# One-head attention on Trainium2: the second context of each pair turned whole on TensorE, the first loaded in both layouts, and the first transfers sent inside the norm

## What is computed

```python
x = x + _L0_xattn_ref(_layernorm(x), ctx_1024, ctx_1024, Wq, bq, Wk, bk, 32, 0)

q = einsum('bld,ed->ble', query, Wq) + bq
k = einsum('bld,ed->ble', key, Wk) + bk
scores = einsum('bqd,bkd->bqk', q, k) / 32
attn = softmax(scores, axis=-1)
return einsum('bqk,bkd->bqd', attn, value)      # key = value = ctx_1024
```

## Time and profile before

| | us |
|---|---|
| median of 3 runs | 3767.55 |
| lowest, highest | 3767.08, 3770.37 |
| the profiled execution | 3748.75 |
| its span (first to last instruction) | 3747.0 |
| mean granted TensorE clock of it (share of full speed) | 0.948 |
| one-head stage in it, from the span's start to the last `add` | 209.5 |

### The profile page before, as it was taken

How to read it: one execution, slowest core, us unless ns; L and a number is a source line. 1 busy time by engine, 2 the same in 40 slices (tenths; PEclk the granted TensorE clock), 3 DMA queues, 4 the chain that set the end, 5 groups by cost and what they waited for, 6 DMA issues and landing times. The chain is left out here.

```text
span 3747.0 us, 96803 instructions
## 1 busy us (share of the span) xinstructions
PE 3314.1 (88%) x40678; PEld 2442.0 (65%) x40678; DVE 2529.9 (68%) x3627; ACT 2085.7 (56%) x3878; POOL 1150.4 (31%) x1140
## 2 busy tenths in 40 slices
PE   8786999999999678999999984689999999999989
PEld 5565677777777566777777762456666666666654
DVE  4653777777774346777777756578878787878751
ACT  3421566556664124656666654366777777676733
POOL 0024222222221352212222200145555545454530
PEclk8987999999999788999999997799999999999989
DMA  7934665565562336545455510100000000000000
GB/s 199 241 101 131 163 172 153 150 173 146 157 173 53 98 103 147 119 122 138 120 123 138 127 44 0 32 25 17 25 17 26 17 25 17 25 17 25 17 4 24
DMA packets 136408, 337.82 MB, mean 90 GB/s; under 512 B 56515, under 2 KB 78603, under 8 KB 135979
## 3 DMA queue, kind: packets, MB, share of 16 engines
q1 hardware_dynamic: 132843, 325.21, 33.6%
q0 software_dynamic: 3136, 6.46, 0.5%
HBM read 166.49 MB, written 17.17 MB: 49 GB/s over the span
## 5 line engine op out<-in xcount | busy, mean ns | idle before, releaser
L2148 POOL TENSOR_TENSOR l_S<-l_S,l_shift 125x448 f32<-125x448 f32 (+1 forms) x416 | 461.3, 1152 | 328.7 <-ACT l_shift L2380 326.2
L1464 ACT ACTIVATE L1a_probs<-ps 125x448 f32<-125x448 f32 x768 | 383.3, 544 | 204.1 <-PE ps L1364 190.6
L1464 ACT ACTIVATE L2a_probs<-ps 125x448 f32<-125x448 f32 x768 | 382.6, 544 | 203.2 <-PE ps L1364 189.6
L1497 DVE TENSOR_REDUCE L2a_chunk_max<-ps 112x1 f32<-112x1000 f32 x256 | 300.9, 1196 | 148.0 <-PE ps L1323 147.6
L1497 DVE TENSOR_REDUCE L1a_chunk_max<-ps 112x1 f32<-112x1000 f32 x256 | 300.9, 1196 | 137.3 <-PE ps L1323 136.8
L2361 ACT ACTIVATE ctx_stats<-ps 125x512 f32<-125x512 f32 (+1 forms) x416 | 247.9, 596 | 179.7 <-PE ps L2206 170.5
L2258 PE MATMUL ps<-l_S,l_z 125*128 125x448 f32 x768 | 344.2, 545 | 0.0
L2425 DVE TENSOR_REDUCE l_norms<-ctx_stats 125x8 f32<-125x512 f32 (+1 forms) x416 | 268.2, 676 | 77.1 <-ACT ctx_stats L2361 77.0
L2451 DVE SCALAR_TENSOR_TENSOR l_S<-ps,l_neg_cols,l_inv_norms 125x448 f32<-125x448 f32 x384 | 256.3, 680 | 81.4 <-PE ps L2227 76.5
L1323 PE MATMUL ps<-L1a_keys,L1a_queries 98*112 98x500 f32 x768 | 264.9, 428 | 47.5 <-DVE L1a_chunk_max L1497 20.8
L1323 PE MATMUL ps<-L2a_keys,L2a_queries 96*112 96x500 f32 x768 | 264.1, 426 | 46.3 <-DVE L2a_chunk_max L1497 20.7
(11 more groups left out here) (494 smaller groups left out, 7074.0 us busy)
## 6 DMA issues: line engine op xcount, KB each, us to landing
L1a_keys<-L1a_k_hi SPq DMA_DIRECT2D x256, 187.5 KB
L2a_keys<-L2a_k_hi SPq DMA_DIRECT2D x256, 187.5 KB, 3.7
L1a_ctx_T<-in_ctx_T SPq DMA_DIRECT2D x32, 750.0 KB, 6.3
xn<-L_valid SPq DMA_DIRECT2D x32, 750.0 KB, 7.8
L1a_keys<-L1a_k_lo SPq DMA_DIRECT2D x128, 187.5 KB
L2a_ctx_T<-in_ctx_T SPq DMA_DIRECT2D x32, 750.0 KB, 6.4
L2a_keys<-L2a_k_lo SPq DMA_DIRECT2D x128, 187.5 KB, 4.1
a_ctx_N<-in_ctx_N SPq DMA_DIRECT2D x32, 672.0 KB
```

The costliest lines, as they stand in the source:

```text
L1464: nc.scalar.activation(probs[t % NPR][:, h * HQ // 2:(h + 1) * HQ // 2], s.ps[0:KP, i % 3, 0:HQ // 2], ACT.Exp).then_inc(probs_made, 1)
L1497: ins = nc.vector.tensor_reduce(chunk_max[:, n, 0:1], product, AX.XY, ALU.max)
L2148: nc.gpsimd.tensor_tensor(S[b % 2][0:r, t, :], S[b % 2][0:r, t, :], shift[0:r, :], ALU.add)\
```

## The change

Three things change in `attention_one_head`.

The first batch of a pair (2j) is loaded in both layouts, `ctx_T` whole (750 KB). Of the second batch (2j+1) only `ctx_N` is loaded; its `ctx_T` is made on the chip whole, in three turns of four tiles, `turn_context(j, k)` for k = 0, 1, 2, each with its copy `take_context(j, k)`. All turns still go through bank 7, so each waits for the copy of the one before it. TensorE makes turn 0 of pair j+1 behind `mix(j-1)`, turn 1 behind `turn_probs(j)` and turn 2 behind `turn_out(j-1)`, just ahead of `scores(j+1)`. ScalarE copies turn 0 behind the exponentials, and turns 1 and 2 behind the three `probs_T` copies. Every chunk of scores now waits for its copy.

Turn 0 of pair j+1 now needs `ctx_N` of batch 2j+3, which SyncE sends last of its pair; before, it needed that of batch 2j+2.

The first contexts are sent from inside the norm's block (`on_sync`) and no longer from the block ahead of it, batch 1's `ctx_N` before batch 0's.

```diff
@@ -287,7 +287,6 @@
 
     PAIRS, NB, NBN = B // 2, 4, 6
-    LOADED = KT - KT // NKC
     QP = 64
     TG = KT // NKC
     with ExitStack() as ctx:
@@ -323,8 +322,7 @@
             sem(n) for n in ("probs_turned", "turned_taken", "mixed", "scaled", "out_turned", "added", "stats_made"))
 
         def load_T(sp, b):
-            sp.dma_start(ctx_T[b % NB][:, 0:LOADED, :],
-                         a["ctx_T"][b, :, 0:LOADED * KP].rearrange("d (t p) -> d t p", t=LOADED))\
+            sp.dma_start(ctx_T[b % NB][:, :, :], a["ctx_T"][b].rearrange("d (t p) -> d t p", t=KT))\
                 .then_inc(T_loaded[b % NB], 16)
 
         def load_N(sp, b):
@@ -338,14 +336,17 @@
                 for dst, src in ((wq[:, :], "L0_WqT"), (wk[:, :], "L0_Wk"), (bias[:, 0:1], "L0_bq"),
                                  (bias[:, 1:2], "L0_bk")):
                     sp.dma_start(dst, a[src]).then_inc(weights_loaded, 16)
-                for b in range(2):
-                    load_T(sp, b)
-                    load_N(sp, b)
 
...
-        norm()
+
+        def load_first(sp):
+            load_T(sp, 0)
+            load_N(sp, 1)
+            load_N(sp, 0)
+
+        norm(on_sync=load_first)
 
         batches = ExitStack()
         block = batches.enter_context(nc.Block())
@@ -355,8 +356,7 @@
             for j in range(1, PAIRS):
                 if j >= 2:
                     sp.wait_ge(scores_made, (j - 2) * NKC + NKC)
-                for b in (2 * j, 2 * j + 1):
-                    load_T(sp, b)
+                load_T(sp, 2 * j)
                 if j >= 3:
                     sp.wait_ge(mixed, j - 3 + 1)
                     sp.wait_ge(stats_made, (j - 2) * 2 * KT)
@@ -380,17 +380,14 @@
             mm.then_inc(qbk_made, 1)
 
             def scores(j):
-                for u in range(2):
-                    b = 2 * j + u
-                    pe.wait_ge(T_loaded[b % NB], 16 * (b // NB) + 16)
+                pe.wait_ge(T_loaded[2 * j % NB], 16 * (2 * j // NB) + 16)
                 if j == 0:
                     pe.wait_ge(qbk_taken, 1)
                     pe.wait_ge(qk_taken, NCH)
                 for k in range(NKC):
                     if j:
                         pe.wait_ge(probs_made, (j - 1) * NKC + k + 1)
-                    if k == NKC - 1:
-                        pe.wait_ge(ctx_taken, 2 * j + 2)
+                    pe.wait_ge(ctx_taken, NKC * j + k + 1)
                     for u in range(2):
                         b = 2 * j + u
                         mm = nc.tensor.matmul(s.ps[QP * u:QP * u + QP, k, 0:KC], qk_pad[:, b, :],
@@ -398,15 +395,17 @@
                                               start=True, stop=True)
                     mm.then_inc(scores_made, 1)
 
-            def turn_context(b):
-
-                pe.wait_ge(N_loaded[b % NBN], 32 * (b // NBN) + 32)
-                if b:
-                    pe.wait_ge(ctx_taken, b)
+            def turn_context(j, k):
+
+                b = 2 * j + 1
+                if k == 0:
+                    pe.wait_ge(N_loaded[b % NBN], 32 * (b // NBN) + 32)
+                if j or k:
+                    pe.wait_ge(ctx_taken, NKC * j + k)
                 else:
                     pe.wait_ge(qk_taken, NCH)
                 for i in range(TG):
-                    mm = nc.tensor.transpose(s.ps[:, 7, i * KP:(i + 1) * KP], ctx_N[b % NBN][:, LOADED + i, :],
+                    mm = nc.tensor.transpose(s.ps[:, 7, i * KP:(i + 1) * KP], ctx_N[b % NBN][:, k * TG + i, :],
                                              s.ident[0:KP, 0:KP])
                 mm.then_inc(ctx_turned, 1)
 
@@ -440,21 +439,23 @@
                 pe.wait_ge(scaled, j + 1)
                 nc.tensor.transpose(s.ps[:, 6, D:2 * D], out[:, :], s.ident[:, :]).then_inc(out_turned, 1)
 
-            for b in range(2):
-                turn_context(b)
+            for k in range(NKC):
+                turn_context(0, k)
             for j in range(PAIRS + 1):
                 if j < PAIRS:
                     scores(j)
                 if j:
                     mix(j - 1)
                 if j + 1 < PAIRS:
-                    turn_context(2 * j + 2)
+                    turn_context(j + 1, 0)
                 if j < PAIRS:
                     turn_probs(j)
                 if j + 1 < PAIRS:
-                    turn_context(2 * j + 3)
+                    turn_context(j + 1, 1)
                 if j:
                     turn_out(j - 1)
+                if j + 1 < PAIRS:
+                    turn_context(j + 1, 2)
 
         @block.scalar
         def _(act):
@@ -462,15 +463,15 @@
                 act.wait_ge(qk_made, c + 1)
                 nc.scalar.activation(qk_pad[:, 8 * c:8 * c + 8, :].rearrange("d b q -> d (b q)"), s.ps[:, 4 + c, :],
                                      ACT.Copy).then_inc(qk_taken, 1)
-            def take_context(b):
-                act.wait_ge(ctx_turned, b + 1)
-                if b >= NB:
-                    act.wait_ge(scores_made, (b - NB) // 2 * NKC + NKC)
-                nc.scalar.activation(ctx_T[b % NB][:, LOADED:KT, :].rearrange("d t p -> d (t p)"), s.ps[:, 7, 0:KC],
-                                     ACT.Copy).then_inc(ctx_taken, 1)
-
-            for b in range(2):
-                take_context(b)
+            def take_context(j, k):
+                act.wait_ge(ctx_turned, NKC * j + k + 1)
+                if j >= 2:
+                    act.wait_ge(scores_made, (j - 1) * NKC)
+                nc.scalar.activation(ctx_T[(2 * j + 1) % NB][:, k * TG:(k + 1) * TG, :].rearrange("d t p -> d (t p)"),
+                                     s.ps[:, 7, 0:KC], ACT.Copy).then_inc(ctx_taken, 1)
+
+            for k in range(NKC):
+                take_context(0, k)
             for j in range(PAIRS):
                 act.wait_ge(shift_made, j + 1)
                 if j:
@@ -480,7 +481,7 @@
                     nc.scalar.activation(probs[:, k * KC:(k + 1) * KC], s.ps[:, k, 0:KC], ACT.Exp, bias=shift[:, 0:1],
                                          accum_out=chunk_sum[:, k:k + 1]).then_inc(probs_made, 1)
                 if j + 1 < PAIRS:
-                    take_context(2 * j + 2)
+                    take_context(j + 1, 0)
                 for k in range(NKC):
                     act.wait_ge(probs_turned, j * NKC + k + 1)
                     if j:
@@ -488,7 +489,8 @@
                     nc.scalar.activation(probs_T[:, k * TG:(k + 1) * TG, :].rearrange("p t q -> p (t q)"),
                                          s.ps[0:KP, 3 + k, :], ACT.Copy).then_inc(turned_taken, 1)
                 if j + 1 < PAIRS:
-                    take_context(2 * j + 3)
+                    take_context(j + 1, 1)
+                    take_context(j + 1, 2)
 
         @block.vector
         def _(dve):
@@ -2587,7 +2589,7 @@
             layer_norm(nc, s, f"norm{phase}", s.x_T, s.xn, **beside)
 
         setup(nc, s, a)
-        attention_one_head(nc, s, a, lambda: normalized(0))
+        attention_one_head(nc, s, a, lambda **beside: normalized(0, **beside))
         mixture(nc, s, a, "L0", lambda **beside: normalized(1, **beside), False)
         heads = ExitStack()
         s.heads_out, s.wo_quad, s.bv_quad, s.out_bias = (
```

## The result

| | before | changed |
|---|---|---|
| median of 14 runs each, us | 3764.41 | 3752.69 |
| lowest to highest | 3758.96 to 3770.37 | 3745.27 to 3763.24 |
| ratio, 95% interval | | 0.9976, 0.9965 to 0.9988 |
| profiled execution | 3748.75 | 3752.43 |
| its one-head stage ends at (last `add`) | 209.52 | 193.53 |

The changed kernel is faster by 0.24% (0.12 to 0.35%), 9.0 us by the ratio and 11.7 by the medians. The forecast was 3753.7 us, 13.9 us under the median of three runs known then (3767.55). On another chip the comparison was made again (`r1_changed_again`, 12 runs against 29): ratio 0.9987, 0.9975 to 1.0000, 4.9 us. The two profiled executions cannot be compared whole: the changed one is 3.7 us longer although its stage ends 16.0 us earlier. Where that lies is the subject of the run `b2_before_again`.

What follows compares the result with a forecast made beforehand. The prediction took the 16 full DMA engines to bound the one-head stage. Its terms, -14.9 - 1.0 + 3.0 - 1.0 = -13.9 us, taken from the median 3767.55, gave 3753.7 us, range 3746.5 to 3762.

Steps and rivals of the forecast that it cites:

- Part 3: Context loads between pairs: the transfer queue stays fed, with 1 to 2 us to spare; costed at nothing, +4 us if dry.
- a queue with gaps: Sign in the profile after, in the one-head stage's transfers, that the claim of a fed stream was wrong.
- Bound of before: One-head stage before: the 16 DMA engines are full, 10.61 us a pair; compute alone would take 8.39.
- Part 1: Context transfers: bytes a pair fall from 2500 to 2250 KB, 9.55 us a pair, -14.9 us over 14 pairs.
- Part 2: Compute cycle with four more transposes and one more copy a pair: grows from 8.39 to 8.95 us, under the stream's 9.55.
- the ring: Compute loop from one pair's scores to the next, through `mix`, turns and copies: 8.95 us a pair.
- turn 2 until the scores: Last term of the compute cycle, the third context turn just ahead of the next scores: 0.4 us.
- Part 4: Both ends of the stage: stream starts 1.0 us earlier, last pair +3.0 us, end -1.0 us.
- The tail: After the last scores: `add` and statistics run during turn 2's wait, so exponentials come sooner, -1.0 us.
- The +3.0 for the last landing: Last pair: from its context's landing to its scores 3.66 us in place of 0.69, +3.0 us once.
- The ring rival: One-head stage: compute, not transfers, sets the pace at 8.95 us a pair, giving 3747.7 us; chance 0.20.
- The clock rival: TensorE stops twice a pair and is granted a lower clock, so slower: 3784 us at 0.7; chance 0.05.

Runs made afterwards that it cites:

- r1_changed_again: The changed kernel, unedited, profiled and timed again on another chip against the kernel before: 3740.16 us against 3747.44, ratio 0.9987.
- b2_before_again: The kernel before, unedited, profiled a second time: its one-head stage's last `add` at 207.54 us, what follows the stage 3548.6 us.
- e10_out_early: Changed kernel with batch 2j+1's `ctx_N` sent first, turn 1 between the `turn_probs` groups and `turn_out` right behind it: 3739.64 us, ratio 0.9980 to before.
- e3_second_first: Changed kernel with `ctx_N` of batch 2j+1 sent ahead of that of batch 2j: 3738.52 us, ratio 0.9979 to before.
- e8_deep: Changed kernel with eight `ctx_N` buffers in place of six, loads issued one pair earlier: mean cycle 9.27 us, last `add` at 188.23.

## Why the prediction was right, and where it was not

The time (3752.69) lies in the range (3746.5 to 3762.0), 1.0 us from the forecast, and faster by over 0.2% was given 0.78. The closeness is luck. The gain was smaller than the 13.9 us forecast, 9.0 by the ratio and 4.9 the second time, and the median of before came 3.1 us lower than the one from which the forecast was taken. In the stage the mean cycle came out right through a bound that the prediction had left out. And the profile's 16.0 us hold 5 us of a better granted clock before the first scores, while the 14 cycles gave 9.2 where 14.9 was forecast. Its own sign for an error in Part 3, a queue with gaps, is there: a DMA share of 0.85, where 0.95 or more was expected. The steps:

- **Bound of before: right.** Without the stream its cycle is 8.35 us (I read 8.39), with it 10.3 and 10.7 on average (`before`, `b2_before_again`).
- **Part 1, -14.9 us: the mean cycle was forecast at 9.55 and came at 9.61, but the reason was wrong.** A queue full of transfers would give 9.18 (251 GB/s in `e10_out_early`). The queue was not full. That 9.55 by bytes and 9.59 by the chain lie side by side is chance.
- **Part 2, the ring: 8.95 forecast, 9.13 measured.** The mis-sized term is the last one, turn 2 until the scores: 0.4 in the sum, 83.12 to 83.70 = 0.58. I had counted a part of the turn's 0.65 as overlapped by what follows; the scores follow 0.58 after its start. The others held: exponentials at 4.00 after the scores (3.93), copy 0 at 5.97, copy spacing 0.48 and 1.43.
- **Part 3 is the step that failed.** I had 10.0 us from a landing to the issue for the pair two further on, and called the queue fed, since `ctx_T` was still under way. I never added the way from that issue to its landing and so never had the chain's length. The legs that I had were well sized (3.85 + 6.36 = 10.2). But the `ctx_T` transfer issued at 77.34 ran alone and fast, and the queue stood nearly empty until the `ctx_N` issued at 80.93 arrived. DMA share (in tenths) and rate from 78 to 91 us in 40 slices of 0.33 us:

```profile
DMA  2958799940039657899999789799699389999830
GB/s 56 161 166 277 295 406 406 369 166 18 37 75 226 132 208 302 359 454 302 303 284 208 139 227 284 227 378 246 151 263 168 92 277 296 296 332 425 332 129 19
```

406 GB/s at 79.6 to 80.3, then 18 to 75 GB/s for a microsecond at 81. And from the issue to the landing it is 9.0 us; so the chain is 19.2 us over two pairs, more than two rings (18.3). I had allowed 4 us for a dry queue, at 0.3 us a pair; against a queue at 9.18 it cost 0.43 a pair, 6 us. `e3_second_first` and `e8_deep` show it from two sides.
- **Part 4.** The norm starts at 7.97 (8.0 forecast). First scores 35.08 and 40.01 (40.3); the difference is the granted clock in the norm, which I had taken over from before's profile. At like clock the third turn cost 1.6 and 1.8 us ahead of the first scores (1.85). The tail is 0.97 shorter (1.0). The +3.0 for the last landing was not paid, as the last pair's context had landed before it was needed.
- **The range's other side.** The ring rival (3747.7) was half true: in eight of 14 cycles the ring is the bound. The clock rival is excluded: from 70 to 170 us 1.00 is granted in both profiles of the changed kernel, 0.97 in both of before. (In the second profile, with the late start, it is 0.93 from 52 to 70 us.) The Trainium skill ("TensorE: Matmul & The Clock Gate", Part 4: PE-mode transpose) has transposes not count as busy in the same way; with four more of them in each pair the granted clock was 1.00 in place of 0.97, so here they cost none.

**What stays open.** The stage gained 16.0 us in the first pair of profiles and 8.3 in the second; of the four pairings of the two profiles of each kernel the mean is 12.2. Paired by like granted clock in the first 27 us they say 10.0 (0.87) and 14.3 (1.00). The timed ratios say 9.0 (4.5 to 13.2) and 4.9 (0 to 9.4). A part may be the start. In before the 5 us of a late start reach the stage's end only as 1.7, beside a scatter of the stream's own of 6 us; in the changed kernel they reach it in full, 6.0. Which start the timed runs had, they do not show. A loss of a few us in the later stages is not excluded. And why the 14 cycles of before differ by 5.7 us is not known; the rate of its full queue from 70 to 170 us was 244 GB/s in one profile and 232 in the other.

## What to carry to other kernels

Fewer bytes go on paying only while the queue stays full. Before counting them, follow one buffer around: landing, use, release, issue, landing, and divide by the number of pairs that the buffers span; that is a bound of its own, and it grows when the released work is moved late or the buffer that is needed first is sent last. Here the order of two transfers was worth 6.8 us of the stage, where the whole change was worth 8 to 16; in the kernel's time, neither more buffers nor the other order has been shown to pay.

## What the runs showed of the hardware that was not expected

The full stream's rate is no constant: 275 GB/s at a share of 1.01 from 52 to 70 us, 244 after that, 251 in `e10_out_early`, 232 at a share of 0.99 in before's second profile. Single slices of 0.33 us reach 406, when `ctx_T` runs alone, and 454. The same 14 cycles of before took 143.8 and 149.5 us. And the same later stages differ by up to 33 us in 3750 between the groups of runs, twice what the whole change brings; so a comparison of a few us has to be made on one chip, or in one stage's trace.
